# Dense attention: the last half sum of a group in step 8 instead of step 7

## The reference, cut to what matters

```python
q, k, v = ...                              # 2 x 16 heads, 2048 x 16 each
attn = einsum('bhnd,bhmd->bhnm', q, k) * hd ** -0.5
attn = attn + spatial_bias
attn = softmax(attn, axis=-1)
out = einsum('bhnm,bhmd->bhnd', attn, v)
```

## Time and profile before

| what | value |
|---|---|
| median of three runs | 2928.17 us (2927.76 to 2928.51) |
| profiled execution | 2928.38 us |
| its span, first to last instruction | 2926.6 us |
| PE, DVE, ACT, POOL busy | 99%, 80%, 76%, 43% of the span |
| granted clock of PE, mean | 0.993 of full speed |

### The profile page before, as it was taken

How to read it: one execution, slowest core, us unless ns; L and a number is a source line. 1 busy time by engine, 2 the same in 40 slices (tenths; PEclk the granted TensorE clock), 3 DMA queues, 4 the chain that set the end, 5 groups by cost and what they waited for, 6 DMA issues and landing times.

```text
span 2926.6 us, 107289 instructions
## 1 busy us (share of the span) xinstructions
PE 2883.0 (99%) x44160; PEld 2025.9 (69%) x44160; DVE 2336.9 (80%) x4346; ACT 2222.5 (76%) x4251; POOL 1265.3 (43%) x2348
## 2 busy tenths in 40 slices
PE   8899999999999999999999999999999999999998
PEld 4467666655667755767657777777777777777776
DVE  7899999999999999999856776777677677767765
ACT  4599999999999999999966666666666666666664
POOL 5432333333333323332345455555555554555554
PEclk9899999999999999999999999999999999999999
DMA  7631111111111111111121111111111111111110
GB/s 233 211 115 41 49 49 45 43 49 49 41 46 49 49 39 48 49 49 39 44 65 45 36 31 37 40 47 44 30 37 33 47 45 36 31 38 39 47 43 5
DMA packets 157393, 154.78 MB, mean 53 GB/s; under 512 B 17794, under 2 KB 130946, under 8 KB 156930
## 3 DMA queue, kind: packets, MB, share of 16 engines
q1 hardware_dynamic: 156930, 148.15, 16.3%
HBM read 89.37 MB, written 58.72 MB: 51 GB/s over the span
## 4 chain that ended last, share of the span: by engine, by line
PE 95%; DVE 2%; POOL 1%; ACT 1%; issue 1%; SPq 0%; DMA 0%; POOLq 0%; DVEq 0%; ACTq 0%
PE banks L1534 29%; PE banks L1492 15%; PE banks L1460 15%; PE banks L1475 14%; PE banks L1601 4%; PE banks L1549 4%; PE banks L1639 4%; PE banks L1568 3%; PE banks L1616 2%; PE banks L1429 1%; PE banks L1626 1%; DVE pair_max L1145 1%; PE banks L1447 1%; POOL row_max L641 1%; PE banks L1714 0%
## 5 line engine op out<-in xcount | busy, mean ns | idle before, releaser
L1145 DVE TENSOR_REDUCE pair_max<-banks 128x1 f32<-128x1024 f32 x1024 | 1212.4, 1214 | 106.9 <-PE banks L1460 76.4
L919 ACT ACTIVATE probs<-banks 128x512 f32<-128x512 f32 x2048 | 1186.5, 599 | 99.3 <-PE banks L1475 13.1
L1475 PE MATMUL banks<-q_aug,k_aug 98*32 98x512 bf16 x8192 | 845.7, 381 | 0.2
L1460 PE MATMUL banks<-k_aug,q_aug 96*32 96x512 bf16 x8192 | 663.0, 383 | 8.5 <-DVE pair_max L1145 3.8
L1492 PE MATMUL banks<-probs,v_cur 128*32 128x256 f32 x8192 | 655.7, 379 | 2.1 <-POOL probs L635 2.0
L1492 PEld LDWEIGHTS banks<-probs,v_cur 128*32 128x32 f32 x8192 | 319.3, 111 | 144.1 <-issue 2.4
L1460 PEld LDWEIGHTS banks<-k_aug,q_aug 96*32 96x32 bf16 x8192 | 276.8, 97 | 188.2 <-DVE pair_max L1145 60.2
L641 POOL TENSOR_SCALAR row_max<-pair_max 128x1 f32<-128x1 f32 x508 | 139.6, 278 | 611.0 <-DVE pair_max L1145 603.1
L1475 PEld LDWEIGHTS banks<-q_aug,k_aug 98*32 98x32 bf16 x8192 | 287.3, 95 | 150.4 <-ACT probs L919 4.7
L1534 PEld LDWEIGHTS banks<-hnT,w_sb 128*64 128x64 f32 (+1 forms) x5632 | 308.5, 137 | 25.1 <-ACT hnT L998 25.1
L1534 PE MATMUL banks<-hnT,w_sb 128*64 128x128 f32 (+1 forms) x5632 | 323.9, 275 | 0.9 <-ACT hnT L998 0.9
(11 more groups left out here) (143 smaller groups left out, 4020.5 us busy)
## 6 DMA issues: line engine op xcount, KB each, us to landing
acc_scratch<-acc_sb SPq DMA_DIRECT2D x128, 256.0 KB, 2.5
heads_win<-acc_scratch SPq DMA_DIRECT2D x512, 64.0 KB
q_aug<-q_parts SPq DMA_DIRECT2D x192, 64.0 KB, 2.2
k_aug<-k_parts SPq DMA_DIRECT2D x192, 64.0 KB, 2.2
q_parts<-parts SPq DMA_DIRECT2D x16, 384.0 KB, 3.1
k_parts<-parts SPq DMA_DIRECT2D x16, 384.0 KB, 4.1
x_in<-in_x SPq DMA_DIRECT2D x10, 512.0 KB, 4.9
xT_scratch<-xnT SPq DMA_DIRECT2D x8, 512.0 KB, 5.4
```

Of the source, the lines that this page charges most:

```text
L919: nc.scalar.activation(probs[:, step % PRING, :], banks[:, ring(h, step), :], ACT.Exp, scale=SCALE).then_inc(prob_ready, 1)
L1145: nc.vector.tensor_reduce(pair_max[:, group % 2, q, half:half + 1], banks[:, 4 + 2 * (t % 2):6 + 2 * (t % 2), :], AX.XY, ALU.max).then_inc ...
L1460: last = nc.tensor.matmul(banks[m:m + CT, 4 + t % 4, :], q_aug[0:TERM_ROWS, b, q * P + m:q * P + m + CT], k_aug[0:TERM_ROWS, b, kq * BANK: ...
L1475: last = nc.tensor.matmul(banks[m:m + CT, ring(h, step), :], k_aug[0:AUG, b, kb * P + m:kb * P + m + CT], q_aug[0:AUG, b, qc * CHUNK:(qc + ...
```

## The change

The last half sum of a group goes from step 7 to step 8. With it SUMS_STEP becomes 8, and the call of `save_sums` is moved from behind the exponential of a step to ahead of it.

```diff
 PV_PLAN = {10: (0, 0, 0), 12: (0, 0, 1), 14: (0, 4, 0), 0: (-1, 4, 1),
-           2: (-1, 8, 0), 4: (-1, 8, 1), 6: (-1, 12, 0), 7: (-1, 12, 1)}
+           2: (-1, 8, 0), 4: (-1, 8, 1), 6: (-1, 12, 0), 8: (-1, 12, 1)}
 HALF = CHUNK // 2
-SUMS_STEP = 7
+SUMS_STEP = 8
...
+                    if kb == SUMS_STEP and group > 0:
+                        save_sums(h, group - 1)
                     act.wait_ge(st_ready, h * STEPS + (step + 1))
 
                     act.wait_ge(pv_done, h * PVH + (1 if step < PRING else (step - PRING) // 4 * 2 + 3))
                     nc.scalar.activation(probs[:, step % PRING, :], banks[:, ring(h, step), :], ACT.Exp,
                                          scale=SCALE).then_inc(prob_ready, 1)
-                    if kb == SUMS_STEP and group > 0:
-                        save_sums(h, group - 1)
```

## The result

The kernel changed took 2945.01 us (median of 4 runs, 2944.11 to 2946.45) beside 2928.15 us for the kernel before (2927.76 to 2928.51). The ratio is 1.0058, with a 95% interval of 1.0043 to 1.0073. Run again in a later session it gave 2946.76 beside 2929.11, ratio 1.0062 (1.0048 to 1.0076). The forecast was 2943.6, in a range of 2936 to 2952.

The account below looks back on a forecast made before the run. PE was taken to bound the dense attention, busy 1308.4 of 1310 us. Waits of 9.8 us (once a head) and 5.6 us (usual groups), 15.4 in all, gave 2943.6 us against the median, range 2936 to 2952.

Parts of the forecast that it names:

- The bound: Dense attention: PE goes without a gap, 48 sets or 10.44 us a group, except 0.32 us once a head.
- The order that does not move: ACT, DVE, POOL and SP: the change leaves their orders of instructions as they were.
- The once-a-head term: Group 4, step 13: later half sum delays POOL's copy of values, then DVE; PE's wait grows 0.65 us, 15 times, 9.8 us.
- POOL's wait: POOL ahead of its copy of values: total wait for PE's half sum grows from 33.2 to about 43 us.
- The term of the usual group: Scores of step 11 wait 0.05 us for ACT's late copy and exponential of step 8; 111 groups, 5.6 us.
- The half sum of step 10: PE, usual group: it wants ACT's copy, ready at 2.16 us for its place at 2.18, so no wait.
- a margin of 1.09 - 0.61 us: ACT's copy and exponential of step 8, usual group: slack said to be used up and overdrawn by 0.05 us.
- The estimate of 0.10 us: Usual group, from the skill page's ACTIVATE costs: PE waits 0.10 us, this term 11 us, sum 2949 us; not adopted.
- B: Only the wait in step 13 of group 4 grows, ACT's chain ends in time; 2938.0 us, chance 0.15.
- C: ACT's exponential follows the copy after 0.52 to 0.59 us; each group waits 0.1 to 0.18 us; 2949 to 2958, chance 0.14.
- D: PE's row unaffected: DVE gets its first pair earlier, POOL works in the gap, neither wait grows; 2928.2 us, chance 0.05.
- E: Faster: evenly spaced pairs of maxima give DVE time, the 15 waits of 0.32 us in step 13 go; 2923.4, chance 0.03.

Follow-up runs that it names:

- Restoring group 4 alone: Changed kernel, but in group 4 of each head the half sum stays in step 7; 2936.36 us, 9.2 us over the kernel before.
- the first experiment: Changed kernel, but in group 4 of a head POOL joins the next group's maxima ahead of copying the next head's values; 2933.58 us.
- half of the copy: Changed kernel, but from the second group on ACT copies only 256 of the 512 columns of the sums; 2938.37 us.

## Why the prediction was right, point by point

**The bound.** PE's row without a gap, 48 sets or 10.44 us a group, was the whole basis, and each experiment comes back to it (10.44 to 10.45) when its waits are gone.

**The order that does not move.** "Ahead of the exponential of step 8" was read as the old place. ACT's part of the change moves nothing in its order of instructions, so what came must come from one half sum on PE; the experiments that undo one link at a time bear this out.

**The once-a-head term: 9.8 forecast.** By the trace 15 × (11.38 - 10.77) = 9.2. POOL's wait was forecast at 43 us and is 43.0. Restoring group 4 alone saved 7.7 us of run time (16.9 to 9.2) and 8.5 over 14 heads of the trace, so 9.1 for 15. The link was 0.61 and not 0.65 since POOL's copy now starts 0.71 us behind the half sum (604.73 to 605.44), before 0.75: by the recorded starts the chain was not quite rigid; the last section has a likely reason.

**The term of the usual group: 5.6 forecast, about 9 measured.** This one was too small by over a third. It was 9.2 us in the runs where it stands alone. Single groups give 10.53 - 10.44 = 0.09; averaged over the usual groups of 14 heads it is 0.08 (10.45 before, 10.53 changed; 10.54 in the repeat), 111 × 0.08 = 8.9. The mechanism held, link for link. Forecast: copy at 1.53, exponential at 1.99, its end at 2.61, scores of step 11 at 2.66. Measured: 594.89 - 593.33 = 1.56, then 2.04, 2.64, and 2.70. Two links were short. The copy starts 0.08 us behind the half sum's recorded end (594.20 + 0.61), where the forecast took the 0.05 that it had read off a set of scores; the half sum's own length, 0.61, was right. And the exponential follows the copy after 0.48, not after the 0.46 of one row at the end. The exponential itself was 0.02 shorter than taken. An overdraft of 0.05, the difference of two sums of about 2.6, cannot be better than its links; 0.09 lies within the bounds that I gave (0 to 0.18). The half sum of step 10, said to "just make it" (2.16 for 2.18), did not: it starts at 2.20.

**A slip on the margin.** The forecast writes "a margin of 1.09 - 0.61 us", 0.48, beside an overdraft of 0.05. But a delay of 0.65 that overdraws by 0.05 means a margin of 0.60. Measured are 0.65 - 0.09 = 0.56 us. The sum did not use the 0.48, so the time forecast is not touched.

**The total is nearer than its terms.** By the traces the forecast had 0.6 us too much once a head and 3.3 too little in the usual groups: 15.4 against 9.2 + 8.9 = 18.1, which is what the two profiled executions differ by. The medians of the runs differ by 16.9, so to be only 1.4 us off there is partly luck.

**The estimate of 0.10 us.** The page "ScalarE: Activation LUTs" of the Trainium skill ("What ACT_TABLE_LOAD costs") gave, for 512 elements, an estimate of 0.61 us for an exponential, 0.52 from start to start, and 2949 us in all. The trace has 0.60, and from start to start 0.49 between exponentials and 0.48 from the copy to the exponential, so the overlap is 0.11 us here (0.60 - 0.49, 0.59 - 0.48) and not the page's 93 ns; the measurement decides. The estimate's wait of 0.10 us a group came out nearer to the measured 0.09 than mine, but through a link that is too long.

**The rivals.** B (only the wait once a head) falls with the waits for L921. C (a dearer restart) falls as a mechanism: 0.48 us, not 0.52 or more; but its lowest wait, 0.10 us, is near the measured 0.09. D and E fall with the result, and the first experiment shows why: the wait of step 13 hangs on POOL's order. E had one true part: the wait of step 13 can go, and the kernel is then faster. But it takes POOL's order, not even spacing: in the kernel changed the pairs of steps 7 and 9 are 1.30 us apart, and that wait is 0.84 us instead of 0.32.

## What to carry to other kernels

When one engine bounds a stage without a gap, moving its work about can win only at places where it waits, so list these waits first (here 0.32 us, once a head) and ask of each by whom it is released. Then, for an item moved later, follow every engine that waits for it until the chain comes back to the bounding engine: a delay within the margin costs nothing (here up to 0.65 us behind the scores of step 7), and one beyond it came near to one to one here, in each turn of the loop. An engine that works in the order of its code passes a wait on to all that stands behind it; an item that waits for something late belongs behind the work that others wait for.

## What the runs showed of the hardware

PE's starts in the profile seem not to be equally far from its real work. In the kernel before, where PE goes hundreds of sets without a wait, the exponential of step 7 begins 0.47 us behind the scores' start in the median group (0.44 in the groups right after the wait of step 13). In the kernel changed, with a wait in each group, it is 0.44 everywhere, and in the version without waits (the kernel before with the maxima joined first) 0.52. The modelled durations move along: the scores of step 13 shown for that version read 0.48 us, those of the kernel changed 0.39. The reading that fits is that the recorded starts run up to 0.08 us ahead of the work, and a true wait puts them right. It would account for the 0.04 us missing in POOL's chain (group 4 before has 0.49 us at its step 7, the kernel changed 0.44), for the 0.08 us by which group 4 reads longer with half of the copy (0.52 at its step 7), and for a part of why a wait of 0.05 us cost 0.06 to 0.07. It was not tested by itself.

The kernel before also spread more in a later session (2926.6 to 2933.7 in 21 runs) than in the first (2927.8 to 2928.5 in 4), so differences under about 3 us between kernels of different sessions are left undecided by the runs here.
